# Record transposes on VectorE in 32x32 blocks, and a third PSUM bank for the edge sums

## The reference, cut to what matters

```python
xs = x[:, :C] @ (W_in2f_s / sqrt(C))                      # a table of 128 + 3*128 columns per node
xv = einsum('nci,cf->nfi', x[:, C:].reshape(n, C, 3), W_in2f_v) / sqrt(C)
sj, vj = xs[idx_j], xv[idx_j]                             # gathered per edge
h = softplus(f_ij @ Wf1 + bf1) - log(2)                   # f_ij: the 20 radial features
W = (h @ Wf2 + bf2) * rcut_ij[:, None]                    # factors per edge
m = products of W with sj, vj and the edge's direction
agg = segment_sum(m, idx_i, num_segments=n)               # sums per target node
x = x + (small matmuls of agg);  x = x + experts(layernorm(x))
```

## Time and profile before

| what | us |
|---|---|
| median of three timed runs | 1792.28 |
| the profiled execution, its own time | 1775.62 |
| its span, first to last instruction | 1773.9 |
| PE, DVE, ACT, POOL busy in the span | 1373.2, 1077.8, 839.3, 746.5 |

### The profile page before, as it was taken

The page is one execution under the profiler, slowest core; times in us unless marked ns, Lnnn a source line. Parts: engine busy times, 40 slices in busy tenths (PEclk is TensorE's granted clock), DMA queues, the critical chain, the costliest instruction groups (busy, mean ns, idle before and its releaser), DMA issues. The chain is left out here.

```text
span 1773.9 us, 27789 instructions
## 1 busy us (share of the span) xinstructions
PE 1373.2 (77%) x7164; PEld 811.7 (46%) x7164; DVE 1077.8 (61%) x2846; ACT 839.3 (47%) x2239; POOL 746.5 (42%) x798
## 2 busy tenths in 40 slices
PE   0787587777877877787777778777778629999997
PEld 0552344444444444444444444444445525665554
DVE  6899466766676667667676766776677752111110
ACT  3689455555555555555555555555555501111111
POOL 3200455555555555555555555555553011112211
PEclk9989799999999999999999999999999859999999
DMA  5142123333323333333333233332333432645531
GB/s 204 46 170 83 47 76 82 93 87 95 98 82 89 86 94 95 92 99 94 87 109 85 82 82 87 82 82 82 82 82 67 141 115 75 184 141 156 171 77 23
DMA packets 65893, 173.20 MB, mean 98 GB/s; under 512 B 14027, under 2 KB 22619, under 8 KB 65213
## 3 DMA queue, kind: packets, MB, share of 16 engines
q0 software_dynamic: 43648, 106.09, 23.2%
q1 hardware_dynamic: 22196, 66.57, 10.5%
HBM read 149.28 MB, written 18.08 MB: 94 GB/s over the span
## 5 line engine op out<-in xcount | busy, mean ns | idle before, releaser
L1060 PE MATMUL PS<-prod,oneh 128*64 128x256 f32 x2064 | 495.6, 391 | 255.4 <-DVE prod L890 149.8
L540 POOL DMA_INDIRECT gath<-table_d,recs x344 | 325.0, 945 | 406.2 <-PE PS L1060 164.3
L666 ACT ACTIVATE oneh<-oneh,recs 128x64 f32<-128x64 f32 x1032 | 283.5, 338 | 422.4 <-DVE oneh L877 387.3
L1060 PEld LDWEIGHTS PS<-prod,oneh 128*64 128x64 f32 x2064 | 274.6, 140 | 446.6 <-issue 226.7
L901 DVE TENSOR_TENSOR region_s<-region_s,PS 128x512 f32 x344 | 235.2, 684 | 327.9 <-remote 318.7
L529 POOL DMA_INDIRECT recs<-rec_d,inv_i x344 | 324.9, 944 | 209.7 <-issue 181.4
L1053 PE MATMUL PS<-prod,oneh 128*64 128x256 f32 x1376 | 364.8, 400 | 0.0
L1041 PE MATMUL PS<-wf_sb,h_t 128*128 128x512 f32 x688 | 310.5, 594 | 0.0
L673 ACT COPY PS<-c_rep 128x512 f32<-128x512 f32 x340 | 198.9, 585 | 92.2 <-DVE prod L890 89.5
L888 DVE TENSOR_TENSOR prod<-PS,gath 128x384 f32<-128x384 f32 x344 | 187.4, 545 | 0.0
L890 DVE TENSOR_TENSOR prod<-PS,gath 128x384 f32<-128x384 f32 x344 | 187.2, 544 | 0.0
(11 more groups left out here) (272 smaller groups left out, 1537.9 us busy)
## 6 DMA issues: line engine op xcount, KB each, us to landing
region_r<-wu SPq DMA_DIRECT2D x16, 512.0 KB
region_r<-wd SPq DMA_DIRECT2D x16, 512.0 KB
region_u<-wu SPq DMA_DIRECT2D x16, 512.0 KB, 4.3
region_u<-wd SPq DMA_DIRECT2D x16, 512.0 KB, 5.4
recs<-rec_d,inv_i POOLq DMA_INDIRECT x344
gath<-table_d,recs POOLq DMA_INDIRECT x344
region_u<-rec_in SPq DMA_DIRECT2D x1, 5168.0 KB, 17.3
rec_d<-region_u SPq DMA_DIRECT2D x1, 5168.0 KB
```

Of the source, the lines that this page charges most:

```text
L540: nc.gpsimd.indirect_dma_start(out=gath[:, t % GRING, :], out_offset=None, in_=table_d, in_offset=bass.IndirectOffsetOnAxis(ap=recs[:, q % ...
L666: last = nc.scalar.activation(oneh[:, slot, 1 + i, :], oneh[:, slot, 0, :], ACT.Copy, scale=recs[:, r, k, R_VEC + i:R_VEC + i + 1])
L1060: return nc.tensor.matmul(to, oneh[:, slot, 1 + i, :], prod[:, slot, P_Q:P_B + i + 1:1 + i, :], start=i == 0, stop=i == 2, skip_group_chec ...
```

## The change

DVE transposes the records of a round, a 128x128 tile, in sixteen 32x32 blocks (`nc.vector.transpose`), straight from SBUF to SBUF, between the second and the third tile's products, for round q + 2. PE's transpose, its semaphore `t_done` and ACT's evacuation are gone. With blocks the edges of a tile stand in other columns than with a full transpose, so `first_layer` writes its four matmuls into strided columns of bank 4, of the same number. Bank 7 becomes a third bank of sums: tile n of the edge stage uses `SUM_BANKS[n % 3]`, and `sum_tile(t)` waits for `flushed` of tile t - 3.

```diff
-SRING = 2
+SRING = 3
+SUM_BANKS = (0, 1, 7)
@@ ScalarE
-                def evacuate_records(q, r):
-                    act.wait_ge(t_done, q + 1)
-                    nc.scalar.copy(rec_t[:, r, :], ps_t).then_inc(rec_t_ready, 1)
@@
-                    scaled_one_hots(t, nxt, 0, 0)
-                    if left >= 2:
-                        evacuate_records(q + 2, (r + 2) % RING)
-                    for k in range(1, QUAD):
+                    for k in range(QUAD):
                         scaled_one_hots(t + k, nxt, k, k)
@@ VectorE
+                def transpose_records(r, body):
+
+                    dve.wait_ge(recs_in[r], 16 * QUAD * body + 16 * QUAD)
+                    nc.vector.transpose(rec_t[:, r, :], recs[:, r].rearrange("p k c -> p (k c)")).then_inc(rec_t_ready, 1)
@@
                     for k in range(QUAD):
                         products(t + k, r, k, k, body)
+                        if k == 1 and left >= 2:
+                            transpose_records((r + 2) % RING, body + (r + 2) // RING)
                     for k in range(QUAD):
-                        flush(t + k, k % SRING, first=isinstance(q, int) and q == k == 0)
+                        flush(t + k, SUM_BANKS[(QUAD * r + k) % SRING], first=isinstance(q, int) and q == k == 0)
@@
                 for k in range(QUAD):
                     one_hot(k, 0, k, k, 0, first=True)
+                transpose_records(0, 0)
                 hidden(0, 0)
+                transpose_records(1, 0)
@@ TensorE
-                def transpose_records(q, r, body):
-                    pe.wait_ge(recs_in[r], 16 * QUAD * body + 16 * QUAD)
-                    hold(pe, rec_t_ready, q + 1, pe_passed)
-                    nc.tensor.transpose(ps_t, recs[:, r].rearrange("p k c -> p (k c)"), ident[:, :]).then_inc(t_done, 1)
-
                 def first_layer(q, r):
 
-                    pe.wait_ge(rec_t_ready, q + 2)
+                    pe.wait_ge(rec_t_ready, q + 1)
                     for k in range(QUAD):
-                        last = nc.tensor.matmul(ps_h[:, k * P:(k + 1) * P], wf1_sb[:, k, :], rec_t[:, r, :],
+                        to = ps_h.rearrange("p (k g e) -> p k g e", k=QUAD, g=QUAD)[:, :, k, :]
+                        last = nc.tensor.matmul(to, wf1_sb[:, k, :], rec_t[:, r, :],
                                                 start=k == 0, stop=k == QUAD - 1, skip_group_check=True)
@@
                     for k in range(QUAD):
-                        sum_tile(QUAD * q + k, k, k % SRING, first=isinstance(q, int) and q == 0 and k < SRING)
-                        if k == 1 and left >= 2:
-                            transpose_records(q + 2, (r + 2) % RING, body + (r + 2) // RING)
+                        sum_tile(QUAD * q + k, k, SUM_BANKS[(QUAD * r + k) % SRING],
+                                 first=isinstance(q, int) and q == 0 and k < SRING)
```

More of the change, by code:

```diff
@@ L230, in build @@
         ps_h = PS[:, 4, :]
-        ps_t = PS[:, 7, 0:P]
         ps_c = PS[:, 5, 0:2 * BUCKETS]
@@ L284, in build @@
         rows_in = [sem(f"rows_in{g}") for g in range(GRING)]
-        t_done = sem("t_done")
         rec_t_ready = sem("rec_t_ready")
@@ L641, in _ @@
                 act.wait_ge(s_folded, 4)
-                act.sem_inc(rec_t_ready, 1)
-                def evacuate_records(q, r):
-                    act.wait_ge(t_done, q + 1)
-                    nc.scalar.copy(rec_t[:, r, :], ps_t).then_inc(rec_t_ready, 1)
                 def size_of_z(q):
@@ L686, in step @@
                     seed(t + 3, 3)
-                    scaled_one_hots(t, nxt, 0, 0)
-                    if left >= 2:
-                        evacuate_records(q + 2, (r + 2) % RING)
-                    for k in range(1, QUAD):
+                    for k in range(QUAD):
                         scaled_one_hots(t + k, nxt, k, k)
-                evacuate_records(0, 0)
                 size_of_z(0)
@@ L696, in _ @@
                 log_of_z(0, first=True)
-                evacuate_records(1, 1)
                 for k in range(QUAD):
@@ L901, in flush, with step @@
                     nc.vector.tensor_tensor(block, block, PS[:, bank, :], ALU.add).then_inc(flushed, 1)
-                def step(q, r, body, ahead=True):
-                    nxt, nbody = (r + 1) % RING, body + (r + 1) // RING
+                def step(q, r, body, left=2):
+                    nxt, nbody, ahead = (r + 1) % RING, body + (r + 1) // RING, left >= 1
                     t = QUAD * q
@@ L924, in _ @@
                 for q in range(BODIES * RING, QUADS):
-                    step(q, q % RING, q // RING, ahead=q < QUADS - 1)
+                    step(q, q % RING, q // RING, left=QUADS - 1 - q)
             @block.tensor
@@ L1076, in step @@
                     for k in range(QUAD):
-                        sum_tile(QUAD * q + k, k, k % SRING, first=isinstance(q, int) and q == 0 and k < SRING)
-                        if k == 1 and left >= 2:
-                            transpose_records(q + 2, (r + 2) % RING, body + (r + 2) // RING)
-                transpose_records(0, 0, 0)
+                        sum_tile(QUAD * q + k, k, SUM_BANKS[(QUAD * r + k) % SRING],
+                                 first=isinstance(q, int) and q == 0 and k < SRING)
                 first_layer(0, 0)
-                transpose_records(1, 1, 0)
                 for r in range(RING):
```

## The result

The kernel after takes 1814.90 us (median of 6 runs, 1804.64 to 1822.4), the kernel before 1792.29 us (6 runs, 1788.46 to 1794.03). The ratio is 1.0125, with a 95% interval of 1.0087 to 1.0162: 1.25% or 22.6 us slower. It lies in the range of 1765 to 1828 us, but the forecast was no change.

What follows compares the result with a forecast made beforehand. It took a 13.28 us cycle of waits, paced by POOL's gathers, as the bound. With 0 for about 82 rounds and -1 us at both ends, 1792.28 - 1 = 1791.3 us was forecast, range 1765 to 1828 us.

Steps and rivals of the forecast that it cites:

- What bounds the kernel: Edge stage: a 13.28 us cycle of waits; tile 3's flush comes 8.69 us after POOL's first gather, whatever PE's tiles do.
- PE's transpose and ACT's copy: Removed from the edge stage's rounds; both lie in idle time, worth 0, at most 0.33 us a round (28 us).
- DVE's transpose: Added on DVE in each round: 0.35 us, with 0.1 and 0.69 us as ends.
- The wait for the record gather: DVE, between the products of tiles 1 and 2, waits 1.0 to 1.4 us for round q + 2's records.
- The third bank and tile 3: PE's sums: tile 2's wait for flush 0 passes to tile 3, which ends at 917.9, just as before.
- The sum: Whole round: 1.5 of 3.98 us of DVE's cover used, 0 for about 82 rounds; -1 us in all, -3 to +3.
- POOL is not stopped: Slower rival: POOL gathers on, the second layer's results come late; 1.87 us a round, 153 us, 1944 us; chance 0.06.
- faster: PE's own work: Rival: PE's completion hangs on PE's own work, so earlier tiles gain 90 us (1700 us) or 8 to 25; chance 0.25.
- the first layer's later start counts: Slower rival: what is held back follows the second layer, 0.5 us a round, 41 us, 1833 us; chance 0.13.
- the transpose lies against POOL: Slower rival: DVE's transpose delays POOL's run of gathers by up to 0.35 us a round, 29 us, 1821 us; chance 0.10.

Runs made afterwards that it cites:

- e10: e8's kernel again (records loaded by plain SyncE DMAs, unsorted, no POOL record gathers), beside a kernel before of 1789.09 us: 1522.05 us, ratio 0.8508.
- e3: Kernel after with DVE's transpose moved into its idle time before tile 3's flush, and two banks of sums: 1791.61 us, ratio 0.9974.
- e9: e6's kernel again (transpose in DVE's idle time, three banks, POOL's added wait for `w_ready`), beside a kernel before of 1789.09 us: 1725.47 us, ratio 0.9641.
- e1: Kernel after with DVE's transpose moved into its idle time before tile 3's flush, three banks kept: 1866.98 us, ratio 1.0414.
- e6: e1's kernel, POOL also waiting for `w_ready` before the gather that needs tile 3, beside a kernel before of 1550.11 us: 1530.25 us, ratio 0.9884.
- e2: Kernel after with two banks of sums instead of three, transpose still between the second and third products: 1834.57 us, ratio 1.0225.
- e13: Kernel after with DVE's transpose behind tile 3's products, beside a kernel before at the low level: 1578.92 us, ratio 1.0202.
- e17: e13's kernel again (kernel after, transpose behind tile 3's products), also at the low level: 1576.52 us.
- e5: Kernel after, POOL also waiting for `w_ready` before the gather that needs tile 3, beside a kernel before of 1550.11 us: 1649.12 us, ratio 1.0649.
- e14: e5's kernel again (kernel after with POOL's added wait for `w_ready`), also at the low level: 1650.47 us.
- e18: e5's kernel once more (kernel after with POOL's added wait for `w_ready`), also at the low level: 1651.45 us.
- e8: e1's kernel with records loaded unsorted by one plain SyncE DMA a round, not POOL gathers, beside a kernel before of 1550.11 us: 1521.80 us.
- e7: e3's kernel, POOL also waiting for `w_ready` before the gather that needs tile 3, beside a kernel before of 1550.11 us: 1535.74 us, ratio 0.9915.

## Why the prediction was wrong

- *What bounds the kernel.* Right for the ordinary round, and borne out by e10: the long wait follows POOL's run of gathers (8.71 us from its first gather to the flush), and with the record gathers gone all but 0.75 us of it is gone. Rounds of 13.28 us are 66 of the 78 counted before, though, and not nearly all.
- *PE's transpose and ACT's copy, worth 0.* Right: e3 is 0.26% below before, with an interval up to 0.9999; its ordinary rounds are no shorter.
- *DVE's transpose, 0.35 us, 0.1 to 0.69.* 0.31 us. The Trainium skill's 311 ns ("VectorE: DVE Perf Modes", section "The three transpose paths") is given for bf16; this trace has 310 ns for fp32.
- *The wait for the record gather, 1.0 to 1.4 us.* 77.8 us in 69 waits, 1.13 us each. Right.
- *The third bank and tile 3.* PE's gaps changed hands as forecast: in the ordinary round shown 0.87 us before tile 2, for the products, and 0.44 us before tile 3, until flush 0 ends at 1025.09. But tile 3's end, in the ordinary rounds of before 8.63 to 8.65 us after the first product (8.79 in one), now scatters from 8.53 to 9.32 us with the record wait. "Just as before" was right as a mean and wrong as a claim on each round.
- ***The sum: "the cycle holds none of the changed steps, so a round stays at 13.28 us and the term is 0 for about 82 rounds".*** This step failed. It holds for 39 of 78 rounds (13.38 us). The moment at which PE's completions come through was taken as one event, fixed by POOL's run. There are two: tile 3's sum, and behind it the second layer. If the first comes through sooner, by 0.7 us and more, POOL goes on, and the second is held for another two gathers. Slack on DVE did not cover that, for what is lost is not DVE's time but POOL's stop. What brings the first through sooner in the six new rounds stays open: their tile 3 ends 8.54 to 8.64 us after the first product, as in ten ordinary rounds (8.53 to 8.64 us).
- *Rival "POOL is not stopped".* The right mechanism at the wrong size: priced for all rounds or none (153 us, 0.06). It came in 14 of 78 rounds and not 6, at 2.7 us each and not 2.2. The earlier trace rows showed it, and the trace of before has one every twelfth round, where POOL is late; it should have been asked how near the other rounds were to it. With POOL's stop enforced (e9) only six rounds of 78 take over 13.6 us.
- *The clock* stood in no term. A held-up round leaves PE idle for 3.3 us and more, and 25 rounds ran cold after that, 1.04 us longer each than the 13.29 us. The trace of before had six such rounds, and the round of the earlier trace rows, from 407.38 to 421.99, is one of them: 14.61 us, its first sums at a granted clock of 0.62.
- *Rival "faster: PE's own work".* At the high level bringing PE's tiles forward is what costs (e1, 75 us). At the low level it is right: e6 is the fastest with the reference's full computation.
- *Rival "the first layer's later start counts"*: an ordinary round is 0.09 us longer, not 0.5 us. *Rival "the transpose lies against POOL"*: POOL's run starts 3.77 us after the first product in the ordinary rounds of both kernels (but for one of 4.07 us before), and a source gather takes 945 ns in both, so no exclusion as in the rule of the Trainium skill ("SBUF — State Buffer", section "Who interferes with whom") is seen.

Why the two costs partly cancel in the square is argued from traces, not shown by a run. The third bank spares PE the wait of e2, and the record wait brings tile 3's end back from 7.35 to 8.5 us and more, where POOL still stops in most rounds. The trace of e1 points the same way: leaving out every twelfth round and the one behind it, all 19 rounds whose tile 3 ended within 7.6 us of the first product were held up, and none of the 47 in which it ended at 8.2 us or later (these were cold, so POOL's run began later in them too). In the kernel after, again without those, 6 of the 25 rounds that ended between 8.50 and 8.65 us were held up and none of the 33 between 8.65 and 9.00 us. But in the kernel before 65 rounds ended at 8.6 us and none was, so how early tile 3 ends is not all. e13 and e17 should have tested it and ran at the other level.

Open is also what holds PE's completions up. It is not simply POOL's run as a whole: in 10 of those 19 rounds of e1 the flush came before the sixth gather of the run had started, as here between the starts of the fifth and the sixth, 263.62 and 264.88 (DVE's timeline):

```profile
264.48 0.69 DVE L895 TENSOR_TENSOR region_s<-region_s,PS 128x512 f32 x1 [1.08 <-remote]
```

Open are, too, what decides between the two levels, and POOL's wait in the kernel after at the high level; at the low one it makes that kernel 6.5% slower than before (e5, e14, e18), and the kernel after itself did not run there.

## What to carry to other kernels

- A wait that ends at another engine's pause is not slack to be spent: ask which signals pass in that pause, in which order, and what happens when the first comes early. Then make the pause explicit, as POOL's wait for `w_ready` does, and only after that free the bank.
- Count a rare bad round in the profile of before, and ask how far the others are from it; a change that leaves the ordinary round alone can double their number.
- Bringing an engine's work forward may cost more than it saves. On PE the short gaps ran together into one (e1: 1.95 us and more before the sums in 70 of 78 rounds, where the kernel before has 1.6 us), and the work behind it ran in part at 1.2 GHz in 49 of them.

## What was not expected of the hardware

- **Two levels of one kernel.** 1785 to 1803 us or 1546 to 1556 us, by session and not by run; chip 4 had a session of each. Without record gathers the two levels fall together (1521.80 and 1522.05 us, e8 and e10). At the low level PE's completions are not held up, and what a change is worth has another sign there: the third bank costs 75 us at the one (e1 against e3) and gains 5.5 us at the other, with POOL's stop (e6 against e7).
- **Completions held up behind indirect gathers.** At the high level tile 3's came 2.4 to 2.6 us after the start of POOL's last gather in ordinary rounds, 1.7 to 1.8 us after it in the six new held-up ones, and 0.2 to 1.8 us after the start of the latest gather in those of e1, though the matmuls had run; without record gathers, and without the sorting that goes with them, the whole kernel is 15% faster.
- **The clock after a gap.** After gaps of 1.94 us and more before the sums these ran in part at 1.2 GHz in some rounds and at full clock in others (in the kernel after 1.98 us was followed by the lower clock and 3.43 us by the full one, in the kernel before 3.56 us by the full one); after shorter gaps, the ordinary ones of 0.6 to 1.7 us among them, always at full clock.
